# Edge stage of a graph-attention and mixture-of-experts kernel: a node tile is finished at a due visit of its own instead of after visit 402, and ScalarE resets and weights the sums

## The reference

```python
x = x + gnn(layernorm(x), W, a_src, a_dst, src, dst)      # x: 6250 x 256, 206250 edges sorted by dst
x = x + ffn(layernorm(x))
# gnn, 4 heads of 64 columns:
z = einsum('ni,hid->nhd', h, W); es = (z * a_src).sum(-1); ed = (z * a_dst).sum(-1)
e = leaky_relu(es[src] + ed[dst], 0.01)
ex = exp(e - segment_max(e, dst)[dst]); denom = segment_sum(ex, dst)
out = segment_sum((ex / denom[dst])[:, :, None] * z[src], dst)
# ffn: gate logits of 16 experts, top 2, softmax of the two, relu(x w1 + b1) w2 + b2,
#      weighted sum, residual, layer norm with gamma and beta
```

## Time and profile before

| | |
|---|---|
| median of 3 runs | 2748.59 us (2746.23 to 2749.81) |
| profiled execution, its own time | 2749.59 us |
| its span, first to last instruction | 2747.9 us |
| mean granted clock of TensorE | 0.83 |
| busy: PE | 1874.9 us (68%) |
| busy: VectorE | 1765.7 us (64%) |
| busy: ScalarE | 721.2 us (26%) |
| busy: GpSimd | 1837.1 us (67%) |
| stage B, first gather to last logits | 79.3 to 2183.9 us |

### The profile page before, as it was taken

One profiled execution on the slowest core, in us unless ns is written; L12 is line 12 of the kernel. 1 busy time (PEld: TensorE's weight loads), 2 busy tenths in 40 slices (PEclk: granted clock), 3 DMA queues, 4 the chain that ended last, 5 costly groups with the idle time before them and its releaser, 6 DMA issues. The chain is left out here.

```text
span 2747.9 us, 51411 instructions
## 1 busy us (share of the span) xinstructions
PE 1874.9 (68%) x9025; PEld 1444.8 (53%) x9026; DVE 1765.7 (64%) x5315; ACT 721.2 (26%) x2906; POOL 1837.1 (67%) x1951
## 2 busy tenths in 40 slices
PE   7366666666666666666665666666577549999997
PEld 5244444444444444444454444444455428999985
DVE  6677667667667667667676666666788574333326
ACT  5111111111111111111111111111455315555557
POOL 0677777777777777777777777777776035555547
PEclk9678788788888877888878787887888659999998
DMA  9455444454545545445555444455454108533328
GB/s 320 122 134 134 131 134 134 134 134 132 134 132 134 134 132 134 132 132 134 134 134 133 134 132 133 134 134 133 131 155 130 36 28 246 181 107 103 106 93 281
DMA packets 183049, 378.36 MB, mean 138 GB/s; under 512 B 38773, under 2 KB 86816, under 8 KB 182410
## 3 DMA queue, kind: packets, MB, share of 16 engines
q0 software_dynamic: 87744, 243.02, 33.2%
q1 hardware_dynamic: 72152, 111.89, 12.7%
q10 hardware_dynamic: 22898, 20.85, 2.8%
HBM read 341.68 MB, written 33.93 MB: 137 GB/s over the span
## 5 line engine op out<-in xcount | busy, mean ns | idle before, releaser
L685 POOL DMA_INDIRECT ring<-z_table,src_idx x1612 | 1543.8, 958 | 511.6 <-issue 476.5
L950 PE MATMUL psMb<-msg,S 128*128 128x260 f32 x3608 | 1206.7, 492 | 512.4 <-DVE msg L833 512.0
L950 PEld LDWEIGHTS psMb<-msg,S 128*128 128x128 f32 x3608 | 829.5, 241 | 697.7 <-DVE msg L833 549.7
L833 DVE TENSOR_TENSOR msg<-ring,psPb 128x1024 f32<-128x1024 f32 x451 | 546.6, 1212 | 0.0
L878 ACT COPY es_edge<-ring 128x16 f32 x451 | 91.8, 204 | 1580.0 <-SPq L633 1550.9
L760 DVE TENSOR_TENSOR earg<-es_edge,dest_sum 128x16 f32<-128x16 f32 x451 | 79.4, 176 | 464.1 <-ACT es_edge L878 441.7
L748 DVE TENSOR_TENSOR S<-iota_f,psPb 128x512 f32<-128x512 f32 x451 | 306.4, 679 | 0.3
L939 PEld LDWEIGHTS psEb<-node_thirds,ST 128*128 128x128 bf16 x1804 | 103.9, 104 | 363.7 <-issue 337.6
L939 PE MATMUL psEb<-node_thirds,ST 128*128 x1804 | 121.4, 180 | 207.4 <-DVE ST L742 111.6
L742 DVE TENSOR_SCALAR ST<-dst_bc,iota_p 128x512 bf16 x451 | 169.3, 375 | 125.4 <-issue 115.4
L1217 POOL DMA_INDIRECT rows_sb<-norm_rows,src_sb x108 | 110.0, 1018 | 168.1 <-DVE src_sb L1294 150.2
(11 more groups left out here) (207 smaller groups left out, 1520.7 us busy)
## 6 DMA issues: line engine op xcount, KB each, us to landing
dst_bc<-dst_rows SPq DMA_DIRECT2D x202, 256.0 KB, 3.5
ring<-z_table,src_idx POOLq DMA_INDIRECT x1612
w_all<-in_L_ffn_w_dram SPq DMA_DIRECT2D x32, 512.0 KB, 5.9
b_sb<-in_L_ffn_b_dram ACTq DMA_DIRECT2D x108, 128.0 KB, 3.2
got<-pair_rows SPq DMA_DIRECT2D x48, 256.0 KB, 4.1
z_table<-z_out SPq DMA_DIRECT2D x49, 130.0 KB, 6.5
norm_rows<-xnb ACTq DMA_DIRECT2D x49, 128.0 KB, 2.4
acc<-in_x_turned_dram SPq DMA_DIRECT2D x12, 512.0 KB, 9.1
```

The source lines that it names most:

```text
L685: nc.gpsimd.indirect_dma_start(ring[:, s, c, :], None, z_table, bass.IndirectOffsetOnAxis(ap=at, axis=0)).then_inc(b_landed[s], 16)
L833: nc.vector.tensor_tensor(msg[:, s % MR, :, 0:D].rearrange("p g (h d) -> p g h d", h=HEADS), ring[:, bass.ds(slot, 1), :, 0:D].rearrange(" ...
L950: last = nc.tensor.matmul(psM[s % 2][:, 0:ROW], S[:, s % MR, c, :], msg[:, s % MR, c, :], start=c == 0, stop=c == G - 1)
```

## The change

- A tile is closed at a **due** visit: its share of the 451 visits, 9.2 per tile, plus four (`DUE`). Batches are of three tiles until tile 44, then two, one and one; spans are pairs of batches until tile 41, then single. In `NORMED` tiles stand four steps apart.
- Whether each tile's last visit lies by its due visit is tested in stage A (`thr[:, 3:5]`, a one-column matmul, `late`). If one does not, one pass more is run, and the sums are taken in the last pass.
- The four long multiplications at the pass's start are gone; ScalarE multiplies the sums of tile i by `decided` in step i, and the first accumulates wait for it (`b_reset`).
- ScalarE's weighted sums go to a PSUM bank `psW` of one tile; VectorE adds it to `xs` tile by tile. The batch's one residual sum, and the weighting of the last batch by VectorE, are gone. ScalarE waits for `b_acc` before it weights and for `b_added` before it overwrites `psW`; VectorE's accumulate waits for `b_scaled` where a tile is being weighted.
- `rden_b` is multiplied by whether this is the last pass, and no longer blended with 1.
- The logits use free columns of the bank of `psT`, so a tile's transpose waits for the logits' sum of the tile before (`b_log`).

```diff
+SLACK = 4
+LADDER = 4
...
+    PACE = VISITS / NT
+    DUE = [min(VISITS, math.ceil((t + 1) * PACE + SLACK)) for t in range(NT)]
...
-            thr = sb(ctx, "thr", [P, 4])
+            thr = sb(ctx, "thr", [P, 5])
+            late = sb(ctx, "late", [P, 1])
...
+                        step(nc.vector.tensor_scalar(thr[:, 3:4], iota_p[:, :], PACE, PACE + SLACK, ALU.mult, ALU.add))
+                        step(nc.vector.tensor_tensor(thr[:, 4:5], thr[:, 2:3], thr[:, 3:4], ALU.is_gt))
...
-                        dve.wait_ge(a_cnt, 2)
+                        dve.wait_ge(a_cnt, 3)
+                        step(nc.vector.tensor_scalar(late[:, :], psA[0][:, 0:1], 1.0, None, ALU.min))
...
-                nc.vector.tensor_scalar(npass_i[:, :], npass_f[:, 1:2], float(PASSES_MAX), None, ALU.min).then_inc(a_passes, 1)
+                nc.vector.scalar_tensor_tensor(out=npass_i[:, :], in0=npass_f[:, 1:2], scalar=float(PASSES_MAX - 1), in1=late[:, :],
+                                               op0=ALU.min, op1=ALU.add).then_inc(a_passes, 1)
...
+                        nc.tensor.matmul(psA[0][:, 0:1], ones[0:NT, :], thr[0:NT, 4:5], start=True, stop=True).then_inc(a_cnt, 1)
...
-        b_fstep = sem("b_fstep"); b_rden = sem("b_rden"); b_scaled = sem("b_scaled"); b_added = sem("b_added")
+        b_fstep = sem("b_fstep"); b_reset = sem("b_reset"); b_rden = sem("b_rden"); b_scaled = sem("b_scaled"); b_added = sem("b_added")
...
-        BATCHES = [range(t, t + BATCH) for t in range(0, NT - NT % BATCH - BATCH, BATCH)]
-        BATCHES.append(range(BATCHES[-1].stop, NT))
+        ENDS = [*range(BATCH, NT - 3, BATCH), NT - 2, NT - 1, NT]
+        BATCHES = [range(lo, hi) for lo, hi in zip([0] + ENDS, ENDS)]
...
-        SPANS = [(n, n + 1) for n in range(0, NB - 2, 2)] + [(n,) for n in range(NB - 2, NB)]
+        SPANS = [(n, n + 1) for n in range(0, NB - 5, 2)]
+        SPANS += [(n,) for n in range(SPANS[-1][-1] + 1, NB)]
...
-        CLOSES = [FULL + tiles.stop - 1 + SUMMED for tiles in BATCHES]
-        WEIGHED = {CLOSES[n] + 3 + max(min(i, 2), 1) - 1: [] for n in range(NB) for i in range(BATCH)}
-        for n in range(NB - 1):
-            for i, t in enumerate(BATCHES[n]):
-                WEIGHED[CLOSES[n] + 3 + max(i, 1) - 1].append(t)
+        CLOSES = [DUE[tiles.stop - 1] - 1 + SUMMED for tiles in BATCHES]
+        WEIGHED = {CLOSES[n] + 3 + 2 * i: (t, n) for n in range(NB) for i, t in enumerate(BATCHES[n])}
+        assert len(WEIGHED) == NT
+        ADDED = [CLOSES[n] + 2 * len(BATCHES[n]) for n in range(NB)]
...
-                NORMED[max([CLOSES[batches[-1]] + 8] + [at + 1 for at in NORMED])] = (t, p)
+                NORMED[max([ADDED[batches[-1]] + 5] + [at + LADDER for at in NORMED])] = (t, p)
...
-        PER_PASS = (b_pstep, b_nodes, b_group, *b_dst, b_rows, b_S, b_ST, b_dest, b_estep, b_arg, b_p, b_msg, b_sum, b_acc, b_es, b_fstep, b_rden,
+        PER_PASS = (b_pstep, b_nodes, b_group, *b_dst, b_rows, b_S, b_ST, b_dest, b_estep, b_arg, b_p, b_msg, b_sum, b_acc, b_es, b_fstep, b_reset, b_rden,
...
-        PASS_STEPS = 12
+        PASS_STEPS = 11
...
+            psW = ps(ctx, "psWb")
...
-            psL = ps(ctx, "psLb")
+            psL = psT[:, D:D + EXPERTS]
...
-                                        (b_fstep, FIN_STEPS), (b_rden, NB), (b_scaled, NT), (b_added, NB), (b_stats, NT), (b_var, len(SPANS)),
+                                        (b_fstep, FIN_STEPS), (b_reset, NT), (b_rden, NB), (b_scaled, NT), (b_added, NT), (b_stats, NT), (b_var, len(SPANS)),
...
-                    pass_step(nc.vector.tensor_scalar(passes_left[:, 2:3], passes_left[:, 1:2], -1.0, 1.0, ALU.mult, ALU.add))
-                    for h in range(HEADS):
-                        nc.vector.tensor_tensor(acc[:, :, h * DH:(h + 1) * DH], acc[:, :, h * DH:(h + 1) * DH],
-                                                       over(decided[:, :, h:h + 1], [P, NT, DH]), ALU.mult)
...
-                                dve.wait_ge(b_acc, FULL + tiles.stop)
+                                dve.wait_ge(b_acc, DUE[tiles.stop - 1])
...
-                                nc.vector.tensor_scalar(rden_b[:, at, :], rden_b[:, at, :], passes_left[:, 1:2], passes_left[:, 2:3],
-                                                        ALU.mult, ALU.add).then_inc(b_rden, 1)
-                                if n == NB - 1:
-                                    dve.wait_ge(b_rden, NB)
-                                    for t in tiles:
-                                        sums = acc[:, t, 0:D].rearrange("p (h d) -> p h d", h=HEADS)
-                                        nc.vector.tensor_tensor(sums, sums, over(rden_b[:, t, :].unsqueeze(2), [P, HEADS, DH]), ALU.mult).then_inc(b_scaled, 1)
-                            if i == CLOSES[n] + 3:
-                                dve.wait_ge(b_scaled, tiles.stop)
-                                nc.vector.scalar_tensor_tensor(out=xs[:, at, :], in0=acc[:, at, 0:D], scalar=passes_left[:, 1:2], in1=xs[:, at, :],
-                                                               op0=ALU.mult, op1=ALU.add).then_inc(b_added, 1)
-                            if i == CLOSES[n] + 3:
-                                dve.wait_ge(b_added, n + 1)
-                                for t in tiles:
-                                    nc.vector.bn_stats(stats[:, t, :], xs[:, t, :]).then_inc(b_stats, 1)
+                                nc.vector.tensor_scalar(rden_b[:, at, :], rden_b[:, at, :], passes_left[:, 1:2], None, ALU.mult).then_inc(b_rden, 1)
+                        if i + 1 in WEIGHED:
+                            t, _ = WEIGHED[i + 1]
+                            dve.wait_ge(b_scaled, t + 1)
+                            nc.vector.tensor_tensor(xs[:, t, :], psW[:, 0:D], xs[:, t, :], ALU.add).then_inc(b_added, 1)
+                            dve.wait_ge(b_added, t + 1)
+                            nc.vector.bn_stats(stats[:, t, :], xs[:, t, :]).then_inc(b_stats, 1)
...
-                            if i == CLOSES[batches[-1]] + 3:
+                            if i == ADDED[batches[-1]]:
...
-                            if i == CLOSES[batches[-1]] + 5:
+                            if i == ADDED[batches[-1]] + 2:
...
-                            nc.vector.tensor_tensor(logits[:, t, :], psL[:, 0:EXPERTS], gate_row[:, :], ALU.add).then_inc(b_log, 1)
+                            nc.vector.tensor_tensor(logits[:, t, :], psL, gate_row[:, :], ALU.add).then_inc(b_log, 1)
...
+                        dve.wait_ge(b_reset, min(v, NT - 1) + 1)
+                        if v + SUMMED in WEIGHED:
+                            dve.wait_ge(b_scaled, WEIGHED[v + SUMMED][0] + 1)
...
-                        for t in WEIGHED.get(i, ()):
-                            n = t // BATCH
-                            if t == BATCHES[n].start:
-                                act.wait_ge(b_rden, n + 1)
+                        if i < NT:
+                            act.wait_ge(b_nodes, 1)
...
-                                sums = acc[:, t, h * DH:(h + 1) * DH]
-                                last = nc.scalar.activation(sums, sums, ACT.Copy, scale=rden_b[:, t, h:h + 1])
+                                sums = acc[:, i, h * DH:(h + 1) * DH]
+                                last = nc.scalar.activation(sums, sums, ACT.Copy, scale=decided[:, i, h:h + 1])
+                            last.then_inc(b_reset, 1)
+                        if i in WEIGHED:
+                            t, n = WEIGHED[i]
+                            act.wait_ge(b_rden, n + 1)
+                            act.wait_ge(b_acc, min(i - SUMMED, VISITS))
+                            if t:
+                                act.wait_ge(b_added, t)
+                            for h in range(HEADS):
+                                last = nc.scalar.activation(psW[:, h * DH:(h + 1) * DH], acc[:, t, h * DH:(h + 1) * DH], ACT.Copy,
+                                                            scale=rden_b[:, t, h:h + 1])
...
-                            if i == CLOSES[batches[-1]] + 6:
+                            if i == ADDED[batches[-1]] + 3:
...
-                            if t:
-                                pe.wait_ge(b_log, t)
...
-                                last = nc.tensor.matmul(psL[:, 0:EXPERTS], xnT[:, t % XN, c * P:(c + 1) * P], gate[:, c, :],
+                                last = nc.tensor.matmul(psL, xnT[:, t % XN, c * P:(c + 1) * P], gate[:, c, :],
...
-                                pe.wait_ge(b_xT, t)
+                                pe.wait_ge(b_log, t)
```

More of the change, by code:

```diff
@@ L23 @@
+import math
 from contextlib import ExitStack
```

## The result

The changed kernel takes **2687.35 us**, median of 4 runs (2686.8 to 2687.85), against 2747.93 for the kernel before (4 runs): ratio 0.9777, 95% interval 0.9765 to 0.9788. The forecast was 2690.5, with a range of 2682 to 2708. The profiled execution took 2686.8 us, and its span is 2685.1.

The account below looks back on a forecast made before the run. GpSimd's stream of 1612 gathers, 1.255 us apart, bounds the edge stage. 9.15 + 18.2 + 6.1 + 27.3 - 2 - 0.6 = 58.1 us off 2749.6, median 2690.5; own range 2683 to 2697, with rivals 2682 to 2708.

Parts of the forecast that it names:

- start, four held gathers: Start of the edge stage: four gathers stand still during VectorE's reset multiplications; without these the stream comes 9.15 us earlier.
- crowded stretch: Last 49 visits, a tile finished in each: 169 gathers return from 1.363 to 1.255 us each, 18.2 us gained.
- spread work: Finish work spread through the gather stream: costs it between 0 and 14 us, taken as 2 us.
- last gather to last sum: End of the edge stage: only tile 47's finish steps remain there, 12 us instead of 18.1, 6.1 us gained.
- tail to the last logits: After the last sum: two tiles left instead of 17, 9.0 us instead of 36.3, 27.3 us gained.
- first stage: Before the gathers: three VectorE steps and a one-column matmul for the late test cost 0 to 0.6 us, taken as 0.6.
- rival A: Closings in the edge stage: crowding is only spread, GpSimd waits for its ring slot; 14 us lost, 2702.5 us; chance 0.12.
- Rival C: Tail: low clock throughout and the last store cost 3 to 5 us, inside the range; chance 0.76 together with the forecast.
- B: Start: first groups' traffic, not `tensor_tensor`, makes the gathers long; the 9.15 us stay, 2699.7 us; chance 0.05.
- D: Edge stage: a tile ends after its due point, all 451 visits run again, about 2105 us more, 4795 us; chance 0.01.
- E: VectorE's accumulate: new waits bite in every tile; slower only if each loses over 1.2 us of the stream; chance 0.02.
- F: Finish of the edge stage: no gain at all, which would need it to be hidden already; no separate chance given.

Follow-up runs that it names:

- run 1: Kernel before, with the mask `decided` copied to PSUM for VectorE's four reset multiplications, which stay: 3514.97 us against 3517.87, ratio 0.9992.
- run 10: Kernel before with only the reset of the sums moved to ScalarE: 2741.05 us, ratio 0.9964.
- run 9: Kernel before with the due visits alone, its batches of three and VectorE reset kept: 2714.57 us, ratio 0.987.
- run 8: Changed kernel with a slack of one visit instead of four, which forces a second pass: 6146.78 us, a single execution.
- run 11: Changed kernel with `psW` in SBUF instead of PSUM and `XN` 3 instead of 4: 3439.63 us against 3531.63, ratio 0.9729.
- run 2: Kernel before with the due visits alone, same kernel as run 9, on a chip with pauses: 3470.13 us, ratio 0.9873.

## Why the prediction was right

The stated range held and so did nearly every term. All by the two profiled executions; "gain" is before less after, in us.

| term | forecast gain | measured gain | how |
|---|---|---|---|
| start, four held gathers | 9.15 | 9.18 | 17th gather after the first: 29.75, then 20.57 |
| crowded stretch | 18.2 | 18.2 | 17th to last gather: 2019.45, then 2001.25, both terms together |
| spread work | -2 | 0 | in the line above |
| last gather to last sum | 6.1 | 6.3 | 18.1, then 11.85 |
| tail to the last logits | 27.3 | 27.7 | 36.3, then 8.6 |
| first stage | -0.6 | -1.4 | first gather at 79.29, then 80.73 |
| after the logits | 0 | 2.9 | span 62.8 shorter, last logits 59.9 earlier |
| sum | 58.1 | 62.8 | span; medians: 60.6 |

**The start.** Right in size and in cause. The long gathers are held by VectorE's multiplications with two SBUF operands (run 1 removes the hold and keeps the work), and the reset on ScalarE gives the 9.15 back by itself (run 10). The cover for it was as reckoned: first landed copy at 91.50, forecast 93 at the latest; first message at 97.07, forecast 97; the 17th gather at 101.30, forecast 99.9, of which 1.4 is the later first gather. The gain hangs on two conditions, no gather held and an early first message. The prediction checks the second only for ScalarE's resets and doesn't say that with the first alone nearly nothing would be won (0.1 us, the estimate at run 1). The Trainium skill's rule (SBUF — State Buffer, Who interferes with whom), that a VectorE instruction with two SBUF inputs blocks a GpSimd one that reads SBUF, agrees with these runs. The same section's note that `tensor_tensor` didn't stall DMA in its probe doesn't hold for these indirect gathers: 3.03 to 3.86 us beside a `tensor_tensor` with both inputs in SBUF, 0.94 or 0.95 beside the same one with an input in PSUM.

**The crowded stretch and its price.** The 18.2 us came back whole, and the 2 us for the spread work were not lost: the middle of the stage costs as before, and no wait for the message is over 0.3 us. This term was mis-sized, 2 for 0, within its stated bounds of 0 and 14. Nine visits of slack between tiles were enough to take it all, so the upper bound of rival A, 14 us, was the crowd's own price and no price of the work. The 18.2 were also not one thing. Before, 4.4 us of it were gathers held by batched sums, and about 14 were idle time, mostly waits for the message, the longest 3.4. With the due visits alone (run 9) the waits mostly go, but holds go on all through the stream, and 8.2 us of the 18.2 come back. The other 10.0 come with the tile-wise form: 6.4 are holds that the short sum in PSUM doesn't cause, and which of its parts removes the 3.6 of waits was not separated.

**Last gather to last sum.** Forecast 12, measured 11.85. The due visits alone give it (11.65 in run 9).

**The tail.** Forecast 9.0, measured 8.6: root at 2119.61, logits of tile 47 at 2121.46, of tile 48 at 2123.98. The due visits alone bring it from 36.3 to 17.2 (run 9), as a batch of four is left; the other 8.6 come with the rest of the change. Of these, 6.0 are the three tiles that follow the first one of the last batch in run 9, one every 2.0 us, so the small last batches have the largest part; no run has them alone. Rival C, the clock: from the last sum to the last logits the granted clock was 0.59, near the lower of the two levels, as it was before (0.56). The rows that the forecast took its steps from were at that level already, so nothing was lost beyond the sum.

**First stage.** Forecast 0.6, measured 1.4 in this pair and 0.7 over thirteen profiles. That is within what one execution scatters: it fits steps that aren't hidden and doesn't show them.

**After the logits.** "Moves as a block" was right within 3 us. From the first issue of the row fetches to the end it took 488.5 us before, 485.4 after, 486.4 and 486.6 in runs 9 and 10, whose program there is the same. I take it as scatter between executions; it isn't shown to be more.

**The parts alone.** Where before takes 2750 us, the reset alone gave 9.2, the due visits with the old batches 35.6; 60.6 - 44.8 = 15.8 us are left. The rest of the change is worth 10.0 in the stream and 8.6 in the tail by the profiles, less about 1 for the late start; that is 1.8 more than the medians leave, and the last stage scatters by as much.

**The rivals.** A: excluded by the middle and the last stretch of the stream. B: excluded by run 1 and by run 10. D: true as a mechanism (run 8), and a slack of two is still enough for this edge list, one is not. The 2.3 visits of margin in the forecast fit that. E: no wait for the reset or the copies stands in front of the accumulate. F: the tail shrank by all that was taken off it. The profiles' gain of 62.8 is 4.7 more than forecast: 2.9 of it is the last stage, 2 the spread work. The forecast's own range, 2683 to 2697, is 7 us to either side of 2690.5, which its "3 us more" and "6 less" don't give; the measured time lies in it.

## What to carry over

A stream that one engine issues is bounded by what delays its issues. Look first for work that can be done in the stream's slack instead of behind it, and count how many microseconds per item the other engines have to spare; here 1.6 us of finish went into 9.7 us of slack, at no cost that the profiles show. When a hold on a shared resource goes, ask what else the long instruction delays: with the hold gone and the work left where it was, the rows leave 0.1 us to gain.

## What the runs showed of the hardware beyond what was expected

A gather is not slowed throughout by VectorE's work on two SBUF operands; it is held only if it **begins** during it. In the kernel before, in run 9 and in run 11, 28 gathers began inside a residual sum of that kind (12, 12 and 4). The 23 that were lengthened ended 0.81 to 0.82 us after the sum's end, whether they had begun 0.1 us into it or late. The other five began in its last 0.14 us and kept their usual length (0.94 to 0.96). In run 9 above the sum ends at 1264.82 + 1.02 = 1265.84 and the gather at 1266.66; in run 11 at 2725.34 and 2726.16. A gather that was already under way wasn't lengthened, and neither was the sum: before has this pair, the gather 0.06 us ahead, with its usual 0.95 us (timeline), and run 2 has eight more, 0.05 to 0.07 us ahead.

```profile
2044.75 0.95 POOL L685 DMA_INDIRECT ring<-z_table,src_idx  x1 [0.30 <-issue]
2044.81 1.00 DVE L803 SCALAR_TENSOR_TENSOR xs<-acc,passes_left,xs 128x768 f32<-128x768 f32 x1
```

So the loss is what is left of the VectorE instruction when the gather begins, less 0.13 us (0.95 - 0.82), and nothing if less than that is left. What the gather does in this first 0.13 us isn't shown; it can't simply need the shared thing for itself so long, since in the pairs above the sum begins within that time and neither is slowed. The prediction's "a gather stands still until the multiplication is over" is this, seen from instructions so long that each gather began inside one; its "0.9 us, a gather's usual length" behind them was 0.82.
